# The Mamba2 scan's input products: from plain float32 to three fp32r passes, with the convolution done in place

## The reference, cut to what matters

```
u = layernorm(u, x_norm_w, x_norm_b)
zxbcdt = einsum('bld,od->blo', u, l2norm(in_proj_w)) * DIM ** (-0.5)
z    = zxbcdt[..., :512]            # gates
xBC  = zxbcdt[..., 512:1152]        # what the convolution reads: x (512), B (64), C (64)
dt   = zxbcdt[..., 1152:1156]       # four step sizes
xBC  = silu(conv1d(xBC, conv_w, 4 taps) + conv_b)
dt   = softplus(dt + dt_bias)
y    = chunked scan(x, dt, A, B, C) + D * x
g    = y * silu(z)
out  = (g * rsqrt(mean(g*g) + eps) * rms_w) @ l2norm(out_proj_w).T
```

## Time and profile before

| | |
|---|---|
| median of 3 runs | 5127.16 us (5111.26 to 5134.68) |
| profiled execution, span | 5138.9 us |
| profiled execution, own time | no figure beside its span; the span stands for it |
| scan stage | from about 3611 to about 4510 us of the span |
| one turn, steady | c = 0: about 54.1 us; c = 1: 50.2; c = 2 and c = 3: 48.5 |
| TensorE busy from 4200 to 4500 us | 297.16 of 300 us |
| VectorE / ScalarE / GpSimd busy there | 238.13 / 235.23 / 127.89 us |

### The profile page before, as it was taken

How to read it: one execution, slowest core, us unless ns; L and a number is a source line. 1 busy time by engine, 2 the same in 40 slices (tenths; PEclk the granted TensorE clock), 3 DMA queues, 4 the chain that set the end, 5 groups by cost and what they waited for, 6 DMA issues and landing times. The chain is left out here.

```text
span 5138.9 us, 109366 instructions
## 1 busy us (share of the span) xinstructions
PE 4706.1 (92%) x35413; PEld 2589.8 (50%) x35413; DVE 4275.5 (83%) x6882; ACT 3471.8 (68%) x6677; POOL 1377.0 (27%) x1279
## 2 busy tenths in 40 slices
PE   5869999999999999999999689999599999955998
PEld 4723333333333333333333267777366666645887
DVE  5779999999999999999999768878677877775554
ACT  2428888888888888888888523223377877734554
POOL 1111111111111111111111133333234443435776
PEclk8969999999999999999999889999699999956999
DMA  4931222212222122221222211111100000044442
GB/s 153 349 67 35 52 52 46 43 35 53 52 46 43 35 53 51 46 43 38 50 54 43 71 40 37 41 45 37 53 21 27 25 23 28 21 156 164 166 160 92
DMA packets 236717, 340.13 MB, mean 66 GB/s; under 512 B 60215, under 2 KB 170034, under 8 KB 227612
## 3 DMA queue, kind: packets, MB, share of 16 engines
q1 hardware_dynamic: 220032, 275.39, 22.3%
q0 software_dynamic: 16192, 58.43, 3.1%
HBM read 205.62 MB, written 136.18 MB: 67 GB/s over the span
## 5 line engine op out<-in xcount | busy, mean ns | idle before, releaser
L719 DVE TENSOR_REDUCE at_mxp<-at_ps_m 128x2 f32<-128x1024 f32 x2092 | 2524.4, 1221 | 70.2 <-PE at_ps_m L772 47.3
L692 ACT ACTIVATE at_prob<-at_ps_s 128x512 f32<-128x512 f32 x4100 | 2227.3, 596 | 323.5 <-PE at_ps_s L762 299.7
L782 PE MATMUL at_ps_o<-at_prob,at_vs 128*32 128x256 f32 x16384 | 1313.1, 392 | 13.9 <-ACT at_osum L698 13.9
L762 PE MATMUL at_ps_s<-at_qs,at_ks 51*128 51x512 f32 x4100 | 1036.7, 500 | 2.7 <-ACT at_prob L692 2.7
L772 PE MATMUL at_ps_m<-at_ks,at_qs 49*128 49x512 f32 x4184 | 859.0, 406 | 49.8 <-DMA at_ks<-t_alibi 34.4
L762 PEld LDWEIGHTS at_ps_s<-at_qs,at_ks 51*128 51x128 f32 x4100 | 384.6, 183 | 853.3 <-ACT at_prob L692 852.8
L782 PEld LDWEIGHTS at_ps_o<-at_prob,at_vs 128*32 128x32 f32 x16384 | 322.9, 108 | 778.2 <-issue 389.7
L564 POOL TENSOR_TENSOR at_total<-at_total,at_minus 128x16 f32<-128x16 f32 x65 | 189.6, 2917 | 1128.4 <-DMA at_total<-at_osum 1128.4
L772 PEld LDWEIGHTS at_ps_m<-at_ks,at_qs 49*128 49x128 f32 x4184 | 403.7, 190 | 73.7 <-DVE at_mxp L719 38.0
L67 DVE TENSOR_TENSOR ex_hidc<-ex_hid,ex_hidc 128x512 fp32r<-128x512 f32 x128 | 158.5, 1250 | 169.6 <-ACT ex_hid L2550 169.6
L1222 PE MATMUL mi_ps_f<-mi_w,mi_act 128*128 128x256 f32 x1024 | 260.1, 399 | 17.4 <-DVE mi_acc L1072 17.1
(11 more groups left out here) (317 smaller groups left out, 6161.6 us busy)
## 6 DMA issues: line engine op xcount, KB each, us to landing
t_parts<-pr_parts SPq DMA_DIRECT2D x64, 512.0 KB, 6.4
ex_w<-in_fw SPq DMA_DIRECT2D x32, 1024.0 KB, 7.4
at_ks<-t_parts SPq DMA_DIRECT2D x102, 256.0 KB
t_buf<-at_blank POOLq DMA_DIRECT2D x64, 384.5 KB, 3.2
at_qs<-t_parts SPq DMA_DIRECT2D x96, 256.0 KB
at_vs<-t_v SPq DMA_DIRECT2D x17, 1024.0 KB, 4.8
ex_rest<-t_buf SPq DMA_DIRECT2D x16, 1026.0 KB, 5.2
t_v<-pr_vaug SPq DMA_DIRECT2D x64, 256.0 KB, 5.6
```

The lines of the kernel that those rows point to most:

```text
L692: nc.scalar.activation(prob[0 if up is None else (t + 1) % 2][:, j, :], ps_s[bank][:, :], ACT.Exp).then_inc(s_read, 1)
L719: nc.vector.tensor_reduce(out[:, s4, k + i, 2 * pair:2 * pair + 2], ps_m[i][:, :, :], AX.X, ALU.max).then_inc(mx_read, 1)
L762: nc.tensor.matmul(ps_s[bank][:, :], ks[s][a:a + QROWS, j // 2, t1 * P:(t1 + 1) * P], qs[s][a:a + QROWS, j // 2, c * T:(c + 1) * T], start ...
L782: last = nc.tensor.matmul(ps_o[32 * j:32 * j + 32, q0:q1], vs[s][:, t, 32 * j:32 * j + 32], prob[t % 2][:, j, q0:q1], start=(t == 0 and ha ...
```

## The change

The input weights are kept twice, as an upper and a lower fp32r part (`winc[0]`, `winc[1]`); the step sizes' four columns stay float32 in `wdt`. Each chunk's normed rows are kept in three forms: `uTc[h][0]` and `uTc[h][1]`, upper and lower fp32r, and one float32 `uT` for the step sizes and for the subtraction. ScalarE evicts each `uT0`, `uT1` twice, once rounding to fp32r and once in float32. GpSimd makes the lower part, two instructions a turn, at the end of its turn. TensorE's `ct` and `z` groups become six fp32r matmuls in place of two float32 ones. The array `cv` goes: the taps are summed in `xs` itself, and the silu works in place. In the setup ScalarE rounds the weights in five pieces and GpSimd subtracts them in five pieces, between its other work.

```
-        win = sb("win", [P, KD, ZX])
+        wdt = sb("wdt", [P, KD, NH])
+        winc = [sb(f"winc{c}", [P, KD, RT * P], F32R) for c in range(2)]
-        uT = [sb(f"uT{h}", [P, KD, T]) for h in range(2)]
+        uT = sb("uT", [P, KD, T])
+        uTc = [[sb(f"uTc{h}{c}", [P, KD, T], F32R) for c in range(2)] for h in range(2)]
-        cv = sb("cv", [P, CTL, T])
...
+                def lower_rows(turn, h, k, name):
+                    pool.wait_ge(a_out, place(turn, name)[0] + 1)
+                    lower_part(nc.gpsimd, uTc[h][1][:, k, :], uT[:, k, :], uTc[h][0][:, k, :]).then_inc(u_cut, 1)
+
+                def lower_weights(j):
+                    pool.wait_ge(win_upper, j + 1)
+                    lower_part(nc.gpsimd, win_part(1, j), win_f[j], win_part(0, j)).then_inc(win_cut, 1)
...
                         gate(i, h, 3, True)
+                        lower_rows((i, c), h, 0, "uT0")
+                        lower_rows((i, c), h, 1, "uT1")
...
                 first_root(0)
                 second_root(0)
+                for j in range(3):
+                    lower_weights(j)
                 first_root(1)
+                for k in range(KD):
+                    lower_rows(None, 0, k, f"uT{k}")
+                for j in range(3, 5):
+                    lower_weights(j)
...
                 second_root(1)
+                for k in range(KD):
+                    lower_rows(None, 1, k, f"vT{k}")
...
-                            last = nc.vector.scalar_tensor_tensor(cv[:, ct, :], xc[h][:, ct, k:k + T], conv_w[:, ct, k:k + 1], cv[:, ct, :], ALU.mult, ALU.add)
+                            last = nc.vector.scalar_tensor_tensor(xs[h][:, ct, :], xc[h][:, ct, k:k + T], conv_w[:, ct, k:k + 1], xs[h][:, ct, :], ALU.mult, ALU.add)
...
-                    nc.scalar.activation(xs[h][:, ct, :], cv[:, ct, :], ACT.Silu).then_inc(silu_done, 1)
+                    nc.scalar.activation(xs[h][:, ct, :], xs[h][:, ct, :], ACT.Silu).then_inc(silu_done, 1)
...
-                    nc.scalar.activation(uT[h][:, k, :], bank[:, :], ACT.Identity, scale=nw[:, k:k + 1], bias=nb[:, k:k + 1]).then_inc(a_out, 1)
+                    nc.scalar.activation(uTc[h][0][:, k, :], bank[:, :], ACT.Identity, scale=nw[:, k:k + 1], bias=nb[:, k:k + 1])
+                    nc.scalar.activation(uT[:, k, :], bank[:, :], ACT.Identity, scale=nw[:, k:k + 1], bias=nb[:, k:k + 1]).then_inc(a_out, 1)
...
+                act.wait_ge(w_read, 5)
+                for j in range(5):
+                    nc.scalar.copy(win_part(0, j), win_f[j]).then_inc(win_upper, 1)
...
                 def conv_inputs(i, h, ct):
+                    if i is None:
+                        pe.wait_ge(win_cut, {4: 1, 0: 2, 1: 2, 2: 3, 3: 3}[ct])
+                    if ct == 4:
+                        pe.wait_ge(u_cut, KD if i is None else KD * (i[0] + 2))
                     bank = into(i, f"ct{ct}")
                     for k in range(KD):
-                        last = nc.tensor.matmul(bank[:, :], win[:, k, DI + ct * P:DI + (ct + 1) * P], uT[h][:, k, :], start=(k == 0), stop=(k == KD - 1))
+                        for n, (a, r) in enumerate(CUTS):
+                            last = nc.tensor.matmul(bank[:, :], winc[a][:, k, DI + ct * P:DI + (ct + 1) * P], uTc[h][r][:, k, :],
+                                                    start=(k == 0 and n == 0), stop=(k == KD - 1 and n == 2))
                     last.then_inc(a_done, 1)
...
-                        last = nc.tensor.matmul(bank[:, :], uT[h][:, k, s * P:(s + 1) * P], win[:, k, 0:DI], start=(k == 0), stop=(k == KD - 1))
+                        for n, (a, r) in enumerate(CUTS):
+                            last = nc.tensor.matmul(bank[:, :], uTc[h][a][:, k, s * P:(s + 1) * P], winc[r][:, k, 0:DI],
+                                                    start=(k == 0 and n == 0), stop=(k == KD - 1 and n == 2))
```

More of the change, by code:

```diff
@@ L1331, in scan_phase @@
         raw_sq = xc_flat[1][:, 0:RT * D].rearrange("p (t f) -> p t f", f=D)
-        cvf = cv[:, :, :].rearrange("p c t -> p (c t)")
-        raw_o = cvf[:, 0:KD * DI].rearrange("p (o f) -> p o f", f=DI)
-        raw_dt = cvf[0:NH, KD * DI:KD * DI + D]
+        xsf = xs[1][:, :, :].rearrange("p c t -> p (c t)")
+        raw_o = xsf[:, 0:KD * DI].rearrange("p (o f) -> p o f", f=DI)
+        raw_dt = xsf[0:NH, KD * DI:KD * DI + D]
         uhf = uh[:, :, :].rearrange("p s f -> p (s f)")
@@ L1346, in scan_phase @@
         v1_done, v2_done, v3_done, uh_done = sem("v1_done"), sem("v2_done"), sem("v3_done"), sem("uh_done")
+        win_upper, win_cut, u_cut = sem("win_upper"), sem("win_cut"), sem("u_cut")
         r1_done, r2_done, r3_done = sem("r1_done"), sem("r2_done"), sem("r3_done")
@@ L1356, in scan_phase @@
         RND = 7
+        WIN_PIECES = [(8, 9), (4, 6), (6, 8), (0, 2), (2, 4)]
+        win_part = lambda c, j: winc[c][:, :, WIN_PIECES[j][0] * P:WIN_PIECES[j][1] * P]
+        win_f = [(osb[0] if j == 0 else sz[1])[:, :, :].rearrange("p s c -> p (s c)")[:, a % 8 * D:a % 8 * D + KD * (b - a) * P].rearrange("p (k c) -> p k c", k=KD)
+                 for j, (a, b) in enumerate(WIN_PIECES)]
         over_h = lambda v: v.unsqueeze(2).to_broadcast([P, NH, P])
@@ L1697, in _ @@
                     if r < 4:
-                        last = nc.vector.tensor_copy(win[:, :, 2 * r * P:(2 * r + 2) * P], bank[:, :].rearrange("p (k c) -> p k c", k=KD))
+                        last = nc.vector.tensor_copy(win_f[{0: 3, 1: 4, 2: 1, 3: 2}[r]], bank[:, :].rearrange("p (k c) -> p k c", k=KD))
                     elif r == 4:
-                        nc.vector.tensor_copy(win[:, :, 8 * P:9 * P], bank[:, 0:KD * P].rearrange("p (k c) -> p k c", k=KD))
-                        last = nc.vector.tensor_copy(win[:, :, RT * P:ZX], bank[:, KD * P:KD * P + KD * NH].rearrange("p (k c) -> p k c", k=KD))
+                        nc.vector.tensor_copy(win_f[0], bank[:, 0:KD * P].rearrange("p (k c) -> p k c", k=KD))
+                        last = nc.vector.tensor_copy(wdt[:, :, :], bank[:, KD * P:KD * P + KD * NH].rearrange("p (k c) -> p k c", k=KD))
                     else:
@@ L1769, in conv_inputs @@
                     bank = take(i, f"ct{ct}")
-                    nc.scalar.activation(cv[:, ct, :], bank[:, :], ACT.Identity, scale=conv_w[:, ct, TAPS - 1:TAPS], bias=conv_b[:, ct:ct + 1])
+                    nc.scalar.activation(xs[h][:, ct, :], bank[:, :], ACT.Identity, scale=conv_w[:, ct, TAPS - 1:TAPS], bias=conv_b[:, ct:ct + 1])
                     nc.scalar.copy(xc[h][:, ct, TAPS - 1:CW], bank[:, :]).then_inc(a_out, 1)
@@ L1924, in steps @@
                         for k in range(KD):
-                            last = nc.tensor.matmul(bank[:, s * NH:(s + 1) * NH], uT[h][:, k, s * P:(s + 1) * P], win[:, k, RT * P:ZX], start=(k == 0), stop=(k == KD - 1))
+                            last = nc.tensor.matmul(bank[:, s * NH:(s + 1) * NH], uT[:, k, s * P:(s + 1) * P], wdt[:, k, :], start=(k == 0), stop=(k == KD - 1))
                     last.then_inc(a_done, 1)
```

2 lines of the change are left out of this document (added).

## The result

| | median | runs | from, to |
|---|---|---|---|
| before | 5122.09 us | 20 | 5111.15, 5141.03 |
| after | 5138.57 us | 20 | 5117.63, 5146.89 |

The ratio is 1.0029, with a 95% interval of 1.0018 to 1.0041: 9 to 21 us slower. The forecast was 5122.5 us, no change.

A forecast was written before the change was run, and what follows sets the result against it. The scan's turn was taken as bound by a VectorE and GpSimd chain up to gT1, then by TensorE; -22.4 + 1.6 + 11.7 + 2.0 + 2.4 = -4.7 us gave 5122.5 us, range 5090 to 5144 (forecast's own range 5105 to 5138).

The forecast's parts named there:

- B: Part of the scan's turn from gT1 to the next own(0), 26.20 us, said to be TensorE's own work.
- B's four groups: Groups z2, z3, ct4, ct0 behind gT1, each 0.35 us cheaper in 16 turns: 22.4 us saved.
- clock: Half-clock stretches after longer TensorE waits at gT1: 11.7 us lost in 12 turns, 2.0 in turns c = 0.
- ScalarE's evictions: Second eviction of each uT, ahead of gT3's copy in the scan: charged 0.1 us a turn, 1.6 us in all.
- A: Part of the scan's turn from own(0) to gT1, 22.30 us, set by VectorE and GpSimd; change worth 0.
- before the loop: Start-up: lower rows and weights, softplus's start and second evictions of vT0, vT1 cost 2.4 us, bounds 0 and 4.5.
- the chain: From own(0) through VectorE's variance and GpSimd's second_root and softplus to gate(1): fixed length, sets the turn's first part.
- the tie of 0.15 us: gT1 starts just after GpSimd's gate(1) ends, 0.13 to 0.26 us in all 16 turns.
- The price of a group: Six fp32r passes take 1.37 us against 1.72 for a float32 group: 0.35 us less, nine groups a turn.
- The rival in which the clock takes it all back: Half-clock stretches behind gT1 in all 12 turns, one more in turns c = 0: 5135 us, slower; chance 0.24.
- GpSimd's lower rows: Two instructions of 1.30 us a turn after gate(3), hidden as gate_root waits for VectorE: worth 0.
- P: Theory in the experiments, not the prediction: fp32r passes themselves bring the loop's added half-clock time, wait or no wait.

The follow-up runs named there:

- after_start: The changed kernel with one more wait: GpSimd begins the lower weights only after VectorE's four normalising instructions of the first chunk; ratio to before 1.0018.
- its copy: The changed kernel, unchanged, profiled a second time: loop of 770.4 us, 105.8 us of it at half clock.
- before_longer: The kernel before with one more term (1/19) in GpSimd's softplus series; ratio to before 1.0043.
- A32: The changed kernel with the loop's five groups ahead of gT1 as float32 instructions again, on the upper parts alone; ratio to before 0.9987.
- after_fill: The changed kernel with a fourth fp32r pass (lower part times lower part) in groups ct1, ct2 and z0 of each turn; ratio to before 1.0038.
- after_short: The changed kernel with GpSimd's softplus series cut to the terms up to 1/9; ratio to before 0.9872.
- before_short: The kernel before with GpSimd's softplus series cut to the terms up to 1/9; ratio to before 0.9946.

## Why the prediction was wrong

The forecast was no change, and the kernel became 9 to 21 us slower. The steps that failed are the two outside the loop: routing, which had no term, and the start. By its steps, with means over the profiles: seven of before's loop, four of after's (after_start, with the same loop, among them), the starts of before's seven (88.8 us) and of after's three (95.9), and routing from the first two of each (243.2 us against 234.5).

| term | forecast | measured |
|---|---|---|
| B's four groups | -22.4 | 15 x -1.28 = -19.2 |
| clock | +13.7 | (414.4 - 15 x 24.92) - (416.8 - 15 x 26.20) = +16.8 |
| ScalarE's evictions | +1.6 | 0 |
| A | 0 | 348.8 - 347.1 = +1.7 |
| before the loop | +2.4 | +7.1 |
| routing | no term | +8.7 |
| sum | -4.7 | +15.1 |

The measured sum is 19.8 us off the forecast. The ratio gives 14.9 us (9 to 21). That the two agree to 0.2 us is luck: B scatters by 13 us between before's profiles and by 15 between after's, which leaves the clock's term some 3.5 us unsure (an estimate, the standard error of the two means).

**A and B.** Right: A is the chain, the tie of 0.15 us is there in every turn, the five groups in it are worth nothing. (Before, the ties were 0.15 to 0.18 us, not up to 0.26.) TensorE's wait was forecast at 1.75 us or more and about 4 at c = 0; it was 1.5 to 2.7 and 4.1. A itself grew a little, at its head. In two turns c = 2 of the first profile VectorE came to `own(0)`'s outputs 2.15 us behind its start, without a wait, where in all 16 turns before it came 1.09 us behind and had waited:

```profile
4185.98 1.05 PE L2015 MATMUL sc_ps_y<-sc_xdt,sc_att 128*128 128x128 f32 x8
...
4188.13 0.69 DVE L1637 TENSOR_TENSOR sc_ysum<-sc_ysum,sc_ps_y 128x512 f32<-128x512 f32 x1
```

There TensorE came to `own(0)` ahead of VectorE, and VectorE set the start of the chain. What held VectorE back in just these turns is not shown; the prediction has no term for it.

**The price of a group.** 0.32 us saved, not 0.35, though both of its sides were mis-read. ct2 takes 1.50 us after (4043.53 to 4045.03), where the mix stage's six passes took 1.37. Before, the same ct2 took 1.82 (4072.81 to 4074.63), where the prediction read 1.72 at a z3:

```profile
4072.81 1.98 PE L1912 MATMUL sc_ps_a<-sc_uT,sc_win 128*128 128x512 f32 x4
4074.63 1.88 PE L1918 MATMUL sc_ps_a<-sc_win,sc_uT 128*128 128x512 f32 x4
```

Right in kind, and the forecast saving was 10% too large. By the formula of the Trainium skill that the prediction weighed (TensorE: Matmul & The Clock Gate, "Back-to-back issue gap"), a group would have saved an estimated 0.42 us; the trace has 0.32, further from it than the row.

**The clock.** The mechanism was right, and the runs show it: waits at gT1 of 1.5 us and more bring half-clock time, and the passes by themselves don't. The size, 13.7 us against 16.8, is right within its scatter. The form was not quite right. The prediction had new stretches that cost 1.63 us each in about seven of the 12 turns. In after's profile five of them had one (six in its copy), but most of these lasted 6.8 us, and a third of the added half-clock time stands at the step-size matmuls later in B, which the prediction had left as they were. The rival in which the clock takes it all back was nearly true, 16.8 of 19.2. That idleness and not the kind of matmul decides agrees with the Trainium skill, the same page, "Part 1: The HAM clock gate", by which the engine is throttled unless activity releases it.

**Before the loop.** Mis-sized, 7.1 for 2.4, beyond the bound of 4.5. VectorE's four one-source instructions took 3.66 us beside GpSimd's subtractions, 1.38 alone, and the prediction saw no such collision. It also let chunk 1's root follow the weights at once. That root stood idle 2.75 us for VectorE's variance (3620.64), which comes behind those four instructions, and the lower rows came behind the root and took 2.88 us for two, not 2.6. ct4 began 42.1 us into the stage against 36.7, 5.4 late for 3.1. (The prediction's own terms sum to 3652.45, 2.7 us late, not to 3652.8.)

**GpSimd's lower rows.** Dearer than forecast, 1.70 us (median of 36) for 1.30, and still hidden: `gate_root` waited for VectorE in all 16 turns, 1.3 us in the turn shown.

**Routing.** This is the step that failed most: the sum took a stage that the diff doesn't touch as fixed. 8.7 us of the 15.1 are there, and no view of the profile before announces it. Without it the change would have cost 6 us, some 5129 us on the forecast's scale. That is inside the forecast's own range of 5105 to 5138, though still on the other side of zero, and there the start's missing 4.7 us weigh most.

**Open.** Why the place of GpSimd's code makes ten scatters wait some 3 us longer. The first stall holds a load of instructions in all ten profiles; eight of the nine behind it don't in after, and VectorE then waits for the scatters' landing in nine turns (10.5 us), which may keep the rhythm up. The Trainium skill (Advanced Engine Details and Errata, "ISA Cache") has an engine's instructions cached in two lines of 256, and the place of a loop could matter by that; but the later stalls hold next to no loads, and by that rule alone they stay unexplained. Also open is how long a wait must be: up to 1.4 us in the turns c = 1 to 3 brought no stretch at gT1 (before_longer, A32), and 1.5 to 2.7 us brought one in 29 of 55 turns. Length alone doesn't decide, as waits of 1.6 to 1.7 us at c = 2 brought none in after_fill. That after_short has 27.3 us at half clock and before_short 17.1 may be a small part of P; one profile each can't tell.

## What to carry to other kernels

A cheaper instruction in a stretch that another engine's chain sets turns into a wait of the cheaper engine, and the wait can cost more than nothing: here the clock took back some seven eighths of what the other stretch saved. Shorten the chain as well (here two terms of a series), and the change pays. Compare stages that the change doesn't touch as well: instructions added in one stage moved the code of the next, for 9 us, and a pad of spare instructions in the kernel before is a cheap test of that.

## What the hardware showed that was not expected

- Spare instructions on one engine ahead of a loop can change the loop's length: 33 on GpSimd cost 9 us in routing (243.7 us against 234.4), and 25 on ScalarE and 196 on TensorE brought no such stalls.
- VectorE's one-source float32 instruction of 128 x 256: 0.35 us alone (1.38 for four), 0.92 beside GpSimd's two-source subtraction (3.66 for four). Moving the subtraction away restored 1.38. The Trainium skill (GPSIMD Engine Reference, "Specifications") says that the two engines share SBUF interfaces, with contention where VectorE runs in a 2-port perf mode or reads two inputs from SBUF. The trace agrees that they contend here and gives the size; which mode VectorE was in, it doesn't show.
- The same subtraction of 128 x 512 on GpSimd took 1.27 to 1.77 us: 1.27 in the two at 3656 to 3659 us of after, with VectorE idle, and up to 1.77 beside VectorE.
- Half-clock stretches of a program don't repeat: the same loop had 37.5 to 68.3 us of them in seven profiles, which gave 410.9 to 424.1 us in B.
- Waits that are met already aren't free in number: 392 of them on TensorE, 196 instructions, delayed TensorE's start in routing by 17 us (41.7 us behind the scan's end against 24.1).
